# Identity transposes ahead of the first load, transposes of A3 and Wr in rows, and the first column started without A3

## The reference

```
x = x + (x W0^T + low-rank term picked by a label)
x = x + x Weff1^T            # Weff1 = quantised(W1 + delta) + delta
x = x + (x W2^T + low-rank term picked by a label)
x = x + (x W3^T + gated mixture of 8 rank-16 experts: Wr routes, A3 (8*16 rows) and B3)
```

## Time and profile before

| | us |
|---|---|
| runs of before | 651.33, 651.79, 652.62 (median 651.79) |
| profiled execution: its own time | 650.38 |
| profiled execution: span of the trace | 648.6 |
| PE busy in it | 626.0 (97%) |
| DVE busy | 334.7 (52%) |
| ACT busy | 173.6 (27%) |
| POOL busy | 67.4 (10%) |

### The profile page before, as it was taken

One profiled execution on the slowest core, in us unless ns is written; L12 is line 12 of the kernel. 1 busy time (PEld: TensorE's weight loads), 2 busy tenths in 40 slices (PEclk: granted clock), 3 DMA queues, 4 the chain that ended last, 5 costly groups with the idle time before them and its releaser, 6 DMA issues.

```text
span 648.6 us, 9236 instructions
## 1 busy us (share of the span) xinstructions
PE 626.0 (97%) x3472; PEld 603.2 (93%) x3472; DVE 334.7 (52%) x615; ACT 173.6 (27%) x315; POOL 67.4 (10%) x143
## 2 busy tenths in 40 slices
PE   6989999978999999999999997999999999999996
PEld 5989999778999999999999797999999999999996
DVE  3479998999887628000112294434343434343432
ACT  3443134344321146111221452111111111111111
POOL 3111100042012000000000041111111111111100
PEclk9999999998999999999999997999999999999999
DMA  9942220380000121100003011121121112110001
GB/s 265 268 129 85 78 66 1 40 268 0 2 1 1 13 22 20 22 1 0 0 6 91 1 33 34 65 66 65 65 65 65 65 65 65 65 65 32 33 34 65
DMA packets 55374, 37.67 MB, mean 58 GB/s; under 512 B 26412, under 2 KB 50988, under 8 KB 55348
## 3 DMA queue, kind: packets, MB, share of 16 engines
q1 hardware_dynamic: 55348, 37.31, 20.4%
HBM read 28.91 MB, written 8.39 MB: 58 GB/s over the span
## 4 chain that ended last, share of the span: by engine, by line
PE 76%; DVE 20%; ACT 2%; issue 1%; DMA 1%; POOL 0%; ACTq 0%; DVEq 0%; SPq 0%; POOLq 0%
PE acc L1065 34%; PE acc L1197 31%; DVE q L837 6%; DVE qtmp L836 4%; PE acc L1185 4%; PE aux L1053 2%; DVE h_lo L972 2%; PE acc L1053 1%; PE acc L1239 1%; DVE w_lo L743 1%; PE acc L1240 1%; DVE a_t L848 1%; DVE a_t L839 1%; DVE a_t L843 1%; DVE q L834 1%
## 5 line engine op out<-in xcount | busy, mean ns | idle before, releaser
L1197 PE MATMUL acc<-h_hi,xt_hi 128*128 128x408 f32 x384 | 99.4, 360 | 3.6 <-DVE b_lo L1036 3.6
L1197 PE MATMUL acc<-h_lo,xt_hi 128*128 128x408 f32 x384 | 95.5, 350 | 0.0
L1197 PE MATMUL acc<-h_hi,xt_lo 128*128 128x408 f32 x384 | 95.0, 349 | 0.0
L1065 PE MATMUL acc<-hg_hi,w_hi 128*128 128x352 f32 (+2 forms) x384 | 88.3, 339 | 6.1 <-DVE hg_lo L863 5.9
L1065 PE MATMUL acc<-hg_lo,w_hi 128*128 128x352 f32 (+2 forms) x384 | 86.8, 334 | 0.0
L1065 PE MATMUL acc<-hg_hi,w_lo 128*128 128x352 f32 (+2 forms) x384 | 85.9, 332 | 0.0
L1065 PEld LDWEIGHTS acc<-hg_hi,w_hi 128*128 128x128 f32 x384 | 67.5, 191 | 7.7 <-issue 6.7
L1197 PEld LDWEIGHTS acc<-h_hi,xt_hi 128*128 128x128 f32 x384 | 67.9, 191 | 5.4 <-issue 3.9
L1197 PEld LDWEIGHTS acc<-h_lo,xt_hi 128*128 128x128 f32 x384 | 72.4, 190 | 0.2
L1197 PEld LDWEIGHTS acc<-h_hi,xt_lo 128*128 128x128 f32 x384 | 72.0, 189 | 0.2
L1065 PEld LDWEIGHTS acc<-hg_lo,w_hi 128*128 128x128 f32 x384 | 68.5, 191 | 0.0
(11 more groups left out here) (176 smaller groups left out, 728.0 us busy)
## 6 DMA issues: line engine op xcount, KB each, us to landing
x_st<-in_x_dram SPq DMA_DIRECT2D x64, 128.0 KB, 2.8
out_dram<-out_sb SPq DMA_DIRECT2D x16, 512.0 KB, 2.6
g<-in_L_cond_W_dram SPq DMA_DIRECT2D x8, 512.0 KB, 7.0
w_st<-in_L_cond_W_dram SPq DMA_DIRECT2D x8, 512.0 KB, 4.7
a_t<-in_L_cond_weight_dram SPq DMA_DIRECT2D x8, 512.0 KB, 5.2
w_raw<-in_L_cond_weight_dram SPq DMA_DIRECT2D x8, 512.0 KB, 3.9
a_raw<-in_L_cond_lora_A_dram SPq DMA_DIRECT2D x5, 128.0 KB, 3.5
a_raw<-in_L_cond_lora_A_dram SPq DMA_DIRECT2D x20, 32.0 KB, 2.0
```

Of the source, the lines that this page charges most:

```text
L1065: last = pe.matmul(acc[0:a.shape[-1], slot, bank * BANK:bank * BANK + c1 - c0], a[:, k, :], b[:, k, c0:c1], start=(at == 0 and n == 0), st ...
L1197: last = pe.matmul(acc[:, slot, bank * BANK:bank * BANK + PART], a[:, slot, k, :], b[:, k, c0:c0 + PART], start=(k == 0 and n == 0), stop= ...
```

## The change

PE issues 14 transposes of the identity, whose results nothing reads, before it waits for the first block of W3. The transposes of A3 and Wr no longer alternate. First come A3's six tiles for blocks 0 to 5 in a row, then Wr's six; the last two tiles of each follow in block 1. Their places in PSUM are the third banks of both slots of `acc`, the second of them used twice. Block 0 is multiplied in two parts: banks 0 and 1 (six matmuls) before W3's block 1 is turned, and bank 2 (three matmuls) after it. SP issues W2's tile 0 ahead of A3 and Wr.

```diff
+        WARM = 14
         def a3_at(bank, k0, k1):
-            return acc[:, 0, bank * BANK:bank * BANK + (k1 - k0) * NR].rearrange("p (k c) -> p k c", k=k1 - k0)
+            return acc[:, min(bank, 1), 2 * BANK:2 * BANK + (k1 - k0) * NR].rearrange("p (k c) -> p k c", k=k1 - k0)
@@ sync
                 if k == 0:
+                    load_w2(0)
                     sp.dma_start(a3_st, A3.rearrange("e r d -> (e r) d")).then_inc(a3_in, 16)
                     sp.dma_start(wr_st, Wr).then_inc(a3_in, 16)
-                    load_w2(0)
-            sp.wait_ge(a3_t, 1)
+            sp.wait_ge(a3_t, 2)
             load_w1(6)
@@ scalar (vector alike)
                     w2_high(0)
-                    act.wait_ge(a3_t, 1)
-                    for bank, (k0, k1) in enumerate(a3_tiles):
+                if k in (0, 1):
+                    act.wait_ge(a3_t, k + 1)
+                    for bank in ((0, 1), (2,))[k]:
+                        k0, k1 = a3_tiles[bank]
                         act.copy(hg_hi[:, k0:k1, C_H:C_LOW2], a3_at(bank, k0, k1)).then_inc(a3_hd, 1)
@@ tensor
-            def tile_of(stage, k, at, slot, pairs):
+            def tile_of(stage, k, at, slot, pairs, banks=(0, 1, 2)):
...
-                last.then_inc(h_used if at < KT - 1 else acc_done, 1)
+                if 2 in banks:
+                    last.then_inc(h_used if at < KT - 1 else acc_done, 1)
...
             pe.wait_ge(made, 2)
+            for _ in range(WARM):
+                turn_tile(acc[:, 0, 2 * BANK:2 * BANK + P], ident[:])
             turn_w3(0)
+
+            def turn_a3(tiles):
+
+                for c0, c1, st in ((0, ER, a3_st), (ER, NR, wr_st)):
+                    for bank in tiles:
+                        k0, k1 = a3_tiles[bank]
+                        for k in range(k0, k1):
+                            last = turn_tile(a3_at(bank, k0, k1)[:, k - k0, c0:c1], st[:, k * P:(k + 1) * P])
+                last.then_inc(a3_t, 1)
+
             pe.wait_ge(a3_in, 32)
-            for bank, (k0, k1) in enumerate(a3_tiles):
-                for k in range(k0, k1):
-                    at = a3_at(bank, k0, k1)[:, k - k0]
-                    turn_tile(at[:, 0:ER], a3_st[:, k * P:(k + 1) * P])
-                    last = turn_tile(at[:, ER:NR], wr_st[:, k * P:(k + 1) * P])
-            last.then_inc(a3_t, 1)
+            turn_a3((0, 1))
+            pe.wait_ge(w_split, 1)
+            tile_of(0, 0, 0, 0, three_pairs(0, 0), (0, 1))
             for k in range(KT):
+                if k == 1:
+                    pe.wait_ge(a3_done, 2)
+                    turn_a3((2,))
                 if k + 1 < KT:
                     turn_w3(k + 1)
                 if k == 0:
-                    pe.wait_ge(w_split, 1)
-                    pe.wait_ge(a3_done, len(a3_tiles))
+                    pe.wait_ge(a3_done, 2)
+                if k == a3_tiles[2][0]:
+                    pe.wait_ge(a3_done, 3)
...
-                tile_of(0, k, k, 0, three_pairs(0, 0))
+                tile_of(0, k, k, 0, three_pairs(0, 0), (0, 1, 2) if k else (2,))
```

More of the change, by code:

```diff
@@ L1063, in tile_of @@
                 for n, (a, b) in enumerate(pairs):
-                    for bank, (c0, c1) in enumerate(thirds(WIDTHS[stage])):
+                    for bank in banks:
+                        c0, c1 = thirds(WIDTHS[stage])[bank]
                         last = pe.matmul(acc[0:a.shape[-1], slot, bank * BANK:bank * BANK + c1 - c0],
@@ L1087, in _ @@
             pe.wait_ge(made, 2)
+            for _ in range(WARM):
+                turn_tile(acc[:, 0, 2 * BANK:2 * BANK + P], ident[:])
             turn_w3(0)
-            pe.wait_ge(a3_in, 32)
-            for bank, (k0, k1) in enumerate(a3_tiles):
-                for k in range(k0, k1):
-                    at = a3_at(bank, k0, k1)[:, k - k0]
-                    turn_tile(at[:, 0:ER], a3_st[:, k * P:(k + 1) * P])
-                    last = turn_tile(at[:, ER:NR], wr_st[:, k * P:(k + 1) * P])
-            last.then_inc(a3_t, 1)
+            def turn_a3(tiles):
+                for c0, c1, st in ((0, ER, a3_st), (ER, NR, wr_st)):
+                    for bank in tiles:
+                        k0, k1 = a3_tiles[bank]
+                        for k in range(k0, k1):
+                            last = turn_tile(a3_at(bank, k0, k1)[:, k - k0, c0:c1], st[:, k * P:(k + 1) * P])
+                last.then_inc(a3_t, 1)
+            pe.wait_ge(a3_in, 32)
+            turn_a3((0, 1))
+            pe.wait_ge(w_split, 1)
+            tile_of(0, 0, 0, 0, three_pairs(0, 0), (0, 1))
             for k in range(KT):
+                if k == 1:
+                    pe.wait_ge(a3_done, 2)
+                    turn_a3((2,))
                 if k + 1 < KT:
```

## The result

The kernel after took 647.49 us (median of 5 runs, 646.33 to 648.41), the kernel before 651.51 (5 runs, 650.20 to 652.62). The ratio is 0.994, 95% interval 0.992 to 0.9959: 4.0 us faster where 1.2 was forecast. Two later series of the same kernel, 12 runs each, gave 649.06 and 649.43 (ratios 0.997, 0.9958 to 0.9983, and 0.9962, 0.9944 to 0.9979). Against the runs of before beside them that is 2.2 us (651.25 - 649.06) and 2.5 us (651.90 - 649.43). All 29 runs of after have a median of 648.94 and a wide spread, 646.3 to 651.4; all of the first five lie in its faster half. So the lasting gain is 2.2 to 2.5 us, and the rest of the 4.0 is luck of those five runs, or of their chip, which no run here tells apart.

What follows compares the result with a forecast made beforehand. PE was taken to bound the opening, then DVE's chain, then PE from 147.71 us. Gains of 0.1 (rearrangement) and 1.1 (earlier clock rise) made 1.2 us, from 651.79 to 650.6; range 648.9 to 652.6.

Steps and rivals of the forecast that it cites:

- What bounds the kernel, and the way from the opening to DVE's chain: PE bounds until W3's last block (30.11 us), then DVE until 147.71; PE gains up to 2.2 us pass entirely.
- All later waits are between engines and move together: After the opening, nothing with a fixed time was to catch the gain, so it would reach the end.
- Loads: Opening queue: W2 at about 6.5 us, A3 with Wr at about 8.2; PE starts A3 at 8.25 instead of 6.98.
- Wr in a row: Opening on PE: a Wr tile in a row taken at 0.20 us at the low clock, 0.12 at the high.
- the rival with 0.39 a tile: Wr's tiles cost as much in a row as beside A3: 1.5 us more, 653.2 us; chance 0.07.
- Low-clock chain: Opening all at the low clock: block 2's turn at 16.3 against 16.38 us, rearrangement worth 0.1 us.
- my own sign, 16 or later: Stated test: block 2's turn at 16 us or later would mean the transposes did nothing.
- The clock in the opening: Clock briefly up after the identity transposes, down around A3, up for good 2.2 us sooner than 15.6; worth 1.1 us.
- my 12.2 to 14.7: Forecast window, in us, for the clock's rise for good in the opening; middle 13.4.
- the term that I had at 1.1 + 0.1: The opening's whole gain: 1.1 us for the earlier clock rise, 0.1 for the rearrangement.
- the clock staying up at the start: Rival: clock stays up after the identity transposes; gain 2.8 us less 0.2, 649.1 us; chance 0.24.
- Transposes not raising the clock: Rival: transposes don't raise the opening's clock, or too weakly; up to 2.2 us lost, 653.9 us; chance 0.10.

Runs made afterwards that it cites:

- the first experiment: The kernel before with only the 14 identity transposes added ahead of W3's first block: 650.47 us, ratio 0.9988 to before.
- its second profile: The kernel before, unchanged, run and profiled once more: 651.25 us.
- the second profile of after: The kernel after, unchanged, run and profiled once more: 649.06 us, ratio 0.997 to before.
- the third profile of after: The kernel after, unchanged, run and profiled a third time: 649.43 us, ratio 0.9962 to before.
- the two experiments at 338 us: Identity transposes added on PE ahead of B3's: three to the kernel before, 650.88 us (ratio 0.9996); four to the kernel after, 649.04 us.

## Why the prediction was wrong

- **What bounds the kernel, and the way from the opening to DVE's chain:** right. Wherever the last block was turned earlier, DVE and PE's restart at 147 moved by the same amount: 28.45 and 146.92 in the first experiment, 29.22 and 147.71 in before, 29.88 and 148.36 in its second profile. No load of B1 or A1 held PE up.
- **"All later waits are between engines and move together":** this is the step that failed. The pause at 389 us is 3.57 long in most profiles, but whether the clock falls in it isn't fixed. I had the fall in the earlier trace rows and used it only as evidence for the opening. In before it comes in about nine runs of ten, and holding the clock is worth 3.0 us; in after it is avoided in about half of the runs and comes late, for 1.5 instead of 2.4 us, in a quarter. No case of mine contained a gain outside the opening.
- **Loads:** the order was right and w_split's end at 9.83 was in the range, but PE could start on A3 at 8.79 instead of 8.25. That 0.5 is nearly half of the 1.2 forecast.
- **Wr in a row:** 0.71 for six loads and 2.25 for twelve instructions, against my 6 x 0.216 + 6 x 0.20 = 2.5. Right; the rival with 0.39 a tile is out.
- **Low-clock chain:** turn of block 2 said at 16.3, measured 16.32. By my own sign, 16 or later, the transposes did nothing for it. I compared with 16.38, from the timeline, where the next matmul overlaps; in the chain it was 16.54. The 0.2 of lead was lost again by the last block, and I had put no loss there.
- **The clock in the opening:** the path was the one forecast, up in the transposes, down in the wait for A3, up again, and the identity transposes alone do raise it. The rise for good came late, though: in the seven profiles with after's opening at 15.7, 15.6, 15.3, 15.3, 16.6, 16.4 and 13.8, only the last of them within my 12.2 to 14.7. This is the second step that failed. With the old opening it came at 15.4 to 17.0 (seven profiles). The last block's turn starts at 28.8 to 29.6 in the first seven, on average 29.3, and at 29.2 to 30.0 in the other seven, on average 29.6. So the traces show 0.3 us for the term that I had at 1.1 + 0.1, and the medians of the runs 0.7 to 0.8, with 1.5 by the ratios.
- **Rivals:** the clock staying up at the start (2.8 us) didn't happen. Its 2.8 rests on a start of block 1's nine matmuls at 17.2 before, and the earlier trace rows have 17.41, so 3.0. Transposes not raising the clock: refuted by the stretch 5.50:8.50 at 1.00 and by W3's block 0 at 1.19 for 1.94; the rule of the Trainium skill (TensorE: Matmul & The Clock Gate, Part 4) that transposes don't count for it doesn't hold for these float32 transposes.

So of the 2.2 to 2.5 us that last, about 0.7 to 0.8 is the opening by the medians, and the remainder, some 1.5 us, the x stage. The second number is a difference and was not measured by itself. That after's gain hangs mostly on the fall at 389 us is shown by filling the pause in both kernels.

Why after avoids the fall more often is not settled, but the profiles say more than that it varies. Take the time from the clock's rise for good in the opening to the start of the pause. In the six profiles that fell within the pause it was 373.1 to 373.5 us (before 389.12 - 15.64 = 373.5, the second profile of after 389.15 - 15.62 = 373.5), and the fall came 375.5 us after the rise in all six. In the four that kept the clock it was 373.6 to 374.0, among them before with three transposes and with four, and in the third profile of after, where the clock fell only behind the restart, 389.18 - 15.27 = 373.9. So the opening may reach that far: what seems to count is how long after the rise PE arrives, and from the turn of the last block to the pause the way was nearly the same in all kernels, 359.5 to 360.4 us where nothing was added between them. From the rise to that turn it was 12.9 to 13.8 us with the old opening and 12.6 to 14.9 with after's, on average 13.3 and 13.8. This spread from one execution to the next is wider than the 0.33 and 0.44 by which the two experiments at 338 us moved the pause, and that may be why both missed: the profile of after with four transposes rose late, at 16.55, and came to 373.4 in spite of them. The nearest two profiles on either side of the border differ by less than 0.1 us, and eleven profiles were sorted after the fact, so this is argued and not shown. Nothing here set the moment of the rise by itself.

## What to carry to other kernels

In this kernel a pause of PE of some 3.5 us between two busy stages cost 2.4 to 3 us more than its length, and whether it did changed from run to run and with edits hundreds of microseconds away. Where a trace shows such a pause, fill it with work that nothing reads before tuning anything else, since otherwise edits are judged by chance. Look at the distribution of runs and at the clock of each, not at the median of five, when a kernel's times fall in groups 1 to 3 us apart. And where an opening waits for its loads, early transposes win little if PE must then wait for the next load, here 2.4 us.

## What the runs showed of the hardware that I had not expected

- The same pause of 3.57 us left the clock up (after without identity transposes), took it down (before, the second profile of after), or took it down 1.4 us after the restart (the third); a pause of 2.97 did both as well.
- Fourteen transposes from 1.59 on raised the clock by 5.5 us, and after an idle stretch of 2.4 us from 6.4 on it was down by 9.
- POOL's casts and DVE's subtractions competed in one of two patterns, 10.90 or 10.30 us for the same eight subtractions, with nothing in the program to choose between them. With POOL held back DVE takes 10.30 as well, so in the second pattern only POOL pays: one cast of 4.79 us, against 0.40 alone.
